# Value projections of a layer ahead of the key and query ones, with the operand splits dealt out anew

## The reference

```python
q = (x @ Wq + bq).reshape(B, T, H, S)        # x is the layer norm of the input
k = (x @ Wk + bk).reshape(B, T, H, S)
v = (x @ Wv + bv).reshape(B, T, H, S)
k = k / jnp.maximum(jnp.linalg.norm(k, axis=-1, keepdims=True), 1e-12)
alpha_val = jax.nn.sigmoid(x @ Walpha + balpha)
beta = jax.nn.softplus(x @ Wbeta + bbeta)
# chunks of 128 tokens: decay masks from cumsum(log(alpha)), attention in a chunk, a state across chunks
...
x = x + attention(layernorm(x))
x = x + down((gelu(gate(y)) * up(y)))        # y = layernorm(x), weights = LUT[codes] * scales
```

## Time and profile before

| quantity | value |
|---|---|
| median of three runs | 1176.11 us |
| profiled execution | 1177.4 us |
| its span (first to last instruction) | 1175.6 us |
| TensorE matmul busy in the span | 1152.5 us, 98% |
| VectorE, ScalarE, POOL busy | 838.0, 394.8, 503.1 us |
| loop T = 4 to 15 of the first stage | from about 13.7 us to 57 us of the span |

### The profile page before, as it was taken

One profiled execution on the slowest core, in us unless ns is written; L12 is line 12 of the kernel. 1 busy time (PEld: TensorE's weight loads), 2 busy tenths in 40 slices (PEclk: granted clock), 3 DMA queues, 4 the chain that ended last, 5 costly groups with the idle time before them and its releaser, 6 DMA issues.

```text
span 1175.6 us, 19512 instructions
## 1 busy us (share of the span) xinstructions
PE 1152.5 (98%) x7756; PEld 757.4 (64%) x7756; DVE 838.0 (71%) x1387; ACT 394.8 (34%) x831; POOL 503.1 (43%) x503
## 2 busy tenths in 40 slices
PE   6999999999989999999999999999999999999998
PEld 3565554656534444777777777777777777777775
DVE  7778554544865664887788778877887787777554
ACT  3343432433332232333333333333333333332221
POOL 3267232322445773425542563366335634462110
PEclk9999999999999999999999999999999999999999
DMA  8012000000010001110011001100110011000111
GB/s 295 2 47 82 22 24 28 19 14 5 20 54 18 19 18 37 33 41 19 19 37 37 19 19 37 37 19 19 37 37 19 19 37 37 19 23 23 37 37 63
DMA packets 22635, 41.94 MB, mean 36 GB/s; under 512 B 2640, under 2 KB 2704, under 8 KB 22544
## 3 DMA queue, kind: packets, MB, share of 16 engines
q1 hardware_dynamic: 22544, 40.70, 10.7%
HBM read 36.46 MB, written 4.23 MB: 35 GB/s over the span
## 4 chain that ended last, share of the span: by engine, by line
PE 90%; DVE 5%; POOL 2%; issue 1%; ACT 1%; DMA 1%; SPq 0%; DVEq 0%; POOLq 0%
PE ps L445 37%; PE ps L472 27%; PE ps L408 14%; PE ps L313 7%; PE ps L282 1%; DVE bigA L774 1%; PE ps L367 1%; POOL WR L1188 1%; DMA WR<-wqkv 1%; PE ps L361 1%; POOL kn_s L1156 1%; PE ps L350 1%; PE ps L374 0%; DVE wf L963 0%; DVE X L887 0%
## 5 line engine op out<-in xcount | busy, mean ns | idle before, releaser
L472 PE MATMUL ps<-WR,ihl_s 128*128 128x512 f16 x816 | 185.9, 379 | 0.0
L408 PE MATMUL ps<-XT,WR 128*128 128x512 f16 x768 | 172.0, 382 | 3.0 <-DVE X L928 3.0
L472 PE MATMUL ps<-WR,vv 128*128 128x512 f16 x720 | 164.7, 379 | 0.0
L445 PE MATMUL ps<-XT,WR 128*128 128x256 f16 x1152 | 157.1, 273 | 0.0
L445 PE MATMUL ps<-REG,WR 128*128 128x256 f16 x1152 | 157.1, 273 | 0.0
L928 DVE SCALAR_TENSOR_TENSOR X<-ps,X 128x512 f32<-128x512 f32 x128 | 88.0, 689 | 79.0 <-PE ps L472 76.9
L408 PEld LDWEIGHTS ps<-XT,WR 128*128 128x128 f16 x768 | 75.4, 98 | 94.7 <-DVE X L928 3.5
L472 PEld LDWEIGHTS ps<-WR,ihl_s 128*128 128x128 f16 x816 | 79.9, 98 | 85.3
L445 PEld LDWEIGHTS ps<-XT,WR 128*128 128x128 f16 x1152 | 112.7, 98 | 33.5
L1172 POOL TENSOR_TENSOR ihl_s<-fw,ihl_s 128x512 f16<-128x512 f32 x51 | 63.5, 1264 | 136.1 <-ACT ihl_s L606 136.1
L445 PEld LDWEIGHTS ps<-REG,WR 128*128 128x128 f16 x1152 | 112.7, 98 | 13.0
(11 more groups left out here) (166 smaller groups left out, 1874.1 us busy)
## 6 DMA issues: line engine op xcount, KB each, us to landing
load<-codes SPq DMA_DIRECT2D x48, 256.0 KB
load<-scales SPq DMA_DIRECT2D x48, 256.0 KB
y<-X SPq DMA_DIRECT2D x16, 256.0 KB, 2.0
bigA<-cla SPq DMA_DIRECT2D x14, 256.0 KB, 3.2
WR<-wqkv SPq DMA_DIRECT2D x3, 1024.0 KB, 10.9
X<-x SPq DMA_DIRECT2D x3, 1024.0 KB, 13.1
X<-x SPq DMA_DIRECT2D x4, 256.0 KB, 3.4
bigC<-bv SPq DMA_DIRECT2D x1, 256.0 KB, 5.8
```

Of the source, the lines that this page charges most:

```text
L408: mm = eng.matmul(bank[:, :], buf[:, wp, o + kt, 128 * j:128 * j + 128], XT[:, xp, kt, 512 * b:512 * b + 512], start=(n == 0), stop=(n == 11))
L445: mm = eng.matmul(half_bank(kind, name), w(wp, kt), x(xp, kt), start=(n == 0), stop=(n == 5))
L472: mm = eng.matmul(PS[bank][:, :], ih[:, ip, 128 * tt:128 * tt + 128], buf[:, wp, 8 + j, :], start=(m == 0), stop=(m == 11))
```

## The change

- The value weights are loaded in four slices, ahead of tiles 2 and 3 of x and of the key weights, each with a semaphore of its own. ScalarE and VectorE split them first.
- TensorE projects the four v tiles of block 0 right after their own turns: turn 0, turn 1, v 0, v 1, turn 2, turn 3, v 2, v 3.
- `QKV_EARLY` keeps 8 entries, k and q of block 0. The steps T = 12 to 15 have no projection. k of head 0 of block 1 moves behind the loop, and k of head 1 takes the place of the fourth v tile in the main loop's first step.
- ScalarE evicts k of block 0 instead of VectorE.
- The split of the query weights goes to POOL: it scales the four slices in place (new line 1152), ScalarE rounds them, and POOL subtracts (new line 1148). Before, VectorE had the subtraction.

```diff
-QKV_EARLY = ([(kind, 0, h) for kind in "kq" for h in range(4)] + [("v", 0, h) for h in range(3)]
-             + [("k", 1, 0)])
+QKV_EARLY = [(kind, 0, h) for kind in "kq" for h in range(4)]
-WORDER = {1: 0, 0: 4, 2: 8}
+WORDER = {2: 0, 1: 4, 0: 8}
...
-    if T + 3 < NT:
+    if T == 0:
+        out.insert(0, ("k", 1, 1))
+    elif T + 3 < NT:
         out.append(("v", (T + 3) // 4, (T + 3) % 4))
...
-                pe.wait_ge(s_hi["n1"], 4 * b + 4)
-                pe.wait_ge(s_lo["n1"], 4 * b + 4)
+                needed = 4 * b + h + 1 if kind == "v" else 4 * b + 4
+                pe.wait_ge(s_hi["n1"], needed)
+                pe.wait_ge(s_lo["n1"], needed)
...
-                    pe.wait_ge(s_wql, WORDER[j] + kt + 1)
+                    if kind == "q":
+                        pe.wait_ge(s_wqlp, kt + 1)
+                    else:
+                        pe.wait_ge(s_wql, WORDER[j] + kt + 1)
...
-            for T in range(4):
+            for T in (0, 2):
                 turn("n1", T)
+                turn("n1", T + 1)
+                qkv("v", 0, T)
+                qkv("v", 0, T + 1)
             for T in range(4, NT):
-                qkv(*QKV_EARLY[T - 4])
+                if T - 4 < len(QKV_EARLY):
+                    qkv(*QKV_EARLY[T - 4])
                 turn("n1", T)
                 logits(T - 4)
             qkv("q", 1, 0)
             for T in range(NT - 4, NT):
                 logits(T)
-            qkv("k", 1, 1)
+            qkv("k", 1, 0)
...
+                elif kind == "k" and b == 0:
+                    ac.wait_ge(s_const, 64)
+                    ac.wait_ge(s_mm["k"], h + 1)
+                    eng.activation(kT[:, 0, h, :], PS[bank_of["k", 0, h]][:, :], ACT.Identity,
+                                   bias=bqk_s[:, 4 + h:5 + h], scale=1.0 / (XS * QS)).then_inc(s_k0, 1)
...
-            for T in range(4):
-                if T == 3:
-                    weights_high(1, range(3))
-                if T >= 1:
-                    turn("n1", T - 1)
-            turn("n1", 3)
-            weights_high(1, [3])
+            weights_high(2, [0, 1])
+            turn("n1", 0)
+            weights_high(2, [2, 3])
+            for T in range(1, 4):
+                turn("n1", T)
             ac.wait_ge(s_const, 64)
             eng.mul(wab_h[:, 0, :, :], wab_f[:, :, :], QS).then_inc(s_wabh, 1)
+            weights_high(1, range(4))
...
-                if T in (5, 9):
-                    weights_high(0 if T == 5 else 2, range(4))
+                if T in (6, 7):
+                    weights_high(0, [2 * T - 12, 2 * T - 11])
                 turn("n1", T)
...
-            for T in range(4):
-                stats("n1", T)
-                if T >= 1:
-                    apply("n1", T - 1)
-                if T >= 2:
-                    turn_low("n1", T - 2)
+            stats("n1", 0)
+            stats("n1", 1)
+            apply("n1", 0)
+            apply("n1", 1)
+            weights_low(2, [0, 1])
+            turn_low("n1", 0)
+            weights_low(2, [2, 3])
+            turn_low("n1", 1)
...
+            project("v", 0, 0)
             turn_low("n1", 2)
             turn_low("n1", 3)
-            weights_low(1, [1, 2, 3])
+            weights_low(1, [0, 1, 2, 3])
+            project("v", 0, 1)
...
+            def weights_low(k):
+                hi, lo = (wq[:, a, k, 0:512] for a in range(2))
+                pl.wait_ge(s_wqh, WORDER[0] + k + 1)
+                eng.tensor_tensor(lo, wsrc[0][:, k, :], hi, ALU.subtract).then_inc(s_wqlp, 1)
+
+            def weights_scaled(k):
+                pl.wait_ge(s_w[0], 16)
+                eng.tensor_scalar(wsrc[0][:, k, :], wsrc[0][:, k, :], QS, None, ALU.mult).then_inc(s_wqs, 1)
...
                 norm_scale("n1", T)
+                if T in (4, 5):
+                    weights_scaled(2 * T - 8)
+                    weights_scaled(2 * T - 7)
+                if T in (7, 8):
+                    weights_low(2 * T - 14)
+                    weights_low(2 * T - 13)
...
                 eng.dma_start(X1[:, T, :], xv[0, :, T, :]).then_inc(s_x[(0, 4, 5, 6)[T]], 16)
+                if T == 1:
+                    for k in range(4):
+                        eng.dma_start(wsrc[2][:, k, :], wv[k, :, 1024:1536]).then_inc(s_wv[k], 16)
             load_w(1)
...
             load_w(0)
-            load_w(2)
```

More of the change, by code:

```diff
@@ L228, in block_kernel @@
         s_w = [sem(f"s_w{j}") for j in range(3)]
+        s_wv = [sem(f"s_wv{k}") for k in range(4)]
+        s_k0, s_wqlp, s_wqs = sem("s_k0"), sem("s_wqlp"), sem("s_wqs")
         s_const, s_out = sem("s_const"), sem("s_out")
@@ L258, in ilo, with evicted @@
             return (s_ilop if on_pool(i) else s_ilov), ILO[i]
+        def evicted(kind, b, h):
+            if kind == "k":
+                return (s_qkv["k"], 4 * b + h - 3) if b else (s_k0, h + 1)
+            return s_qkv[kind], 4 * b + h + 1
         def x1(T):
@@ L297, in qkv @@
             def qkv(kind, b, h):
-                pe.wait_ge(s_hi["n1"], 4 * b + 4)
-                pe.wait_ge(s_lo["n1"], 4 * b + 4)
-                j, done = "qkv".index(kind), 4 * b + h + 1
-                bank = bank_of[kind, b, h] = banks.take(pe, (s_qkv[kind], done))
+                needed = 4 * b + h + 1 if kind == "v" else 4 * b + 4
+                pe.wait_ge(s_hi["n1"], needed)
+                pe.wait_ge(s_lo["n1"], needed)
+                j = "qkv".index(kind)
+                bank = bank_of[kind, b, h] = banks.take(pe, evicted(kind, b, h))
                 n = 0
@@ L336, in head @@
                 pe.wait_ge(s_qkv["q"], 4 * b + 4)
-                pe.wait_ge(s_qkv["k"], 4 * b + 4)
+                pe.wait_ge(*evicted("k", b, 3))
                 free = [(s_ss, T + 1)] + ([(s_kw, 3 * b + c + 1)] if c < 3 else [])
@@ L536, in weights_high @@
             def weights_high(j, ks):
-                ac.wait_ge(s_w[j], 16)
                 for k in ks:
-                    eng.mul(wq[:, 0, k, 512 * j:512 * j + 512], wsrc[j][:, k, :], QS).then_inc(s_wqh, 1)
+                    if j == 0:
+                        ac.wait_ge(s_wqs, k + 1)
+                    else:
+                        ac.wait_ge(s_wv[k] if j == 2 else s_w[j], 16)
+                    eng.mul(wq[:, 0, k, 512 * j:512 * j + 512], wsrc[j][:, k, :], QS if j else 1.0).then_inc(s_wqh, 1)
             def project(kind, b, h):
@@ L622, in dq_mul @@
                     if g == 0:
-                        ac.wait_ge(s_wql, 12)
+                        ac.wait_ge(s_wql, 8)
+                        ac.wait_ge(s_wqlp, 4)
                     if g == 1:
@@ L683, in snapshots @@
                 eng.copy(s5b, half_bank(kind, "P5")).then_inc(s_snap, 1)
-            for T in range(4):
-                if T == 3:
-                    weights_high(1, range(3))
-                if T >= 1:
-                    turn("n1", T - 1)
-            turn("n1", 3)
-            weights_high(1, [3])
+            weights_high(2, [0, 1])
[3 more added lines that the diff above has]
+                turn("n1", T)
             ac.wait_ge(s_const, 64)
             eng.mul(wab_h[:, 0, :, :], wab_f[:, :, :], QS).then_inc(s_wabh, 1)
+            weights_high(1, range(4))
             for T in range(4, NT):
-                if T > 4:
+                if 0 <= T - 5 < len(QKV_EARLY):
                     project(*QKV_EARLY[T - 5])
-                if T in (5, 9):
-                    weights_high(0 if T == 5 else 2, range(4))
+                if T in (6, 7):
+                    weights_high(0, [2 * T - 12, 2 * T - 11])
                 turn("n1", T)
@@ L782, in weights_low @@
             def weights_low(j, ks):
-                dv.wait_ge(s_w[j], 16)
                 for k in ks:
+                    dv.wait_ge(s_wv[k] if j == 2 else s_w[j], 16)
                     hi, lo = (wq[:, a, k, 512 * j:512 * j + 512] for a in range(2))
@@ L797, in project @@
                                              ALU.add).then_inc(s_qkv["v"], 1)
-                elif kind == "k":
+                elif kind == "k" and b >= 1:
                     dv.wait_ge(s_const, 64)
@@ L993, in combine @@
                                   ALU.add).then_inc(s_comb, 1)
-            for T in range(4):
-                stats("n1", T)
-                if T >= 1:
-                    apply("n1", T - 1)
-                if T >= 2:
-                    turn_low("n1", T - 2)
+            stats("n1", 0)
[6 more added lines that the diff above has]
+            turn_low("n1", 1)
+            stats("n1", 2)
+            stats("n1", 3)
+            apply("n1", 2)
             apply("n1", 3)
-            weights_low(1, [0])
+            project("v", 0, 0)
             turn_low("n1", 2)
             turn_low("n1", 3)
-            weights_low(1, [1, 2, 3])
+            weights_low(1, [0, 1, 2, 3])
+            project("v", 0, 1)
             dv.wait_ge(s_const, 64)
@@ L1014, in _ @@
                 apply("n1", T)
[L1015 to L1020, removed]
+                if T < 6:
```

(4 more changed lines are left out.)

## The result

The changed kernel takes 1186.52 us (median of four runs, 1186.16 to 1187.65), against 1175.57 us (median of four, 1174.48 to 1176.43) for the kernel before: 1.009 times as long, 95% interval 1.0076 to 1.0105, some 11 us slower. The forecast was 1186.5. Its profiled execution took 1186.5 us, with a span of 1184.6.

The account below looks back on a forecast made before the run. It took the loop to be bound by TensorE (3.33 us a step) and an equally long ring through three engines (3.32). Terms 6.3 + 1.1 + 3.0 = 10.4 us, added to the median 1176.11, gave 1186.5 us; range 1180.5 to 1190.

Parts of the forecast that it names:

- The front: Start of the kernel up to turn 11: v projections placed ahead make it 7.1 us later; bounds 4.4 and 8.1.
- The ring: Steps T = 12 to 15: waits through three engines keep 3.32 us a step; 12.5 us against 13.3, 0.8 back.
- POOL: Query split on POOL, steps T = 7 and 8: wait 0.85 us plus slowed apply 0.25, 1.1 together; bounds 0 and 2.5.
- The clock: TensorE's clock falls in the thinned tail: turns 0.9 us, projection behind turn 15 2.1, 3.0 in all; bounds 0 and 6.5.
- the wait inside the first q projection: Sign at step T = 8: TensorE waits 0.5 to 1 us on POOL inside that projection.
- the projection behind turn 15: Sign behind the loop: this projection takes 4.5 us or more where it was 2.61; 2.6 would mean the clock holds.
- The delay was passed on behind `head(0)`: Behind the loop: gates, head(0) and all that follows hang on turn 15; everything behind head(0) keeps its old durations.
- the rival "no change": Main loop slack takes up the delay, or a much quicker front nearly balances it: 1176 us, chance 0.04.
- the one in which the clock holds: Tail: TensorE's clock stays up, so 6.3 + 1.1 = 7.4 us slower, 1183.5 us; chance 0.37.
- the one in which the bare steps run at TensorE's pace: Steps T = 12 to 15 take 2.9 us, turn 15 starts at 52.9: faster, 1172.8 us; chance 0.04.
- the one of a queue stuck on POOL: A norm_scale stuck behind query slices loses up to 2.4 us in each of two steps: 1190 us; chance 0.06.

Follow-up runs that it names:

- mix: Against the kernel before: v of two tiles first, two other projections at T = 12 and 13, apply one tile ahead; 1175.28 us, 0.9987 (twelve extra matmuls: 1174.24 us, 0.9981).

## Why the prediction was right

The sum of 10.4 us was made of terms that can be read off one by one, up to the 48 logits, where the trace has 10.1.

- **The front**, forecast 7.1 us. The first v at 9.0 was 9.20, the second's end at 16.9 was 17.00, v 2 at 18.9 was 18.93, and the first k at 24.1 was 24.11. Turn 11 lies 7.77 us later than before; 0.5 of that is POOL's, and 7.2 the front's.
- **The ring**, forecast 12.5 us at the upper clock for the four bare steps. They took 13.18 with turns slowed by 0.45 us at T = 13 and 14, which is 12.3 without that: 1.0 us less than before, where the forecast had 0.8. Opening it took the stretch to 6.4 us and, with POOL out of the way, the ratio to 1.0017: shown by experiment, not only by the rows.
- **POOL**, forecast 1.1 us, is the term that was too large: 0.5 by the trace and by undoing it. The wait in the first q projection was 0.26 us, not 0.85 (the step before had been delayed by 0.26 through an `apply` slowed to 0.80, which gave POOL time). The price of a scaled slice, taken as 1.2 us, was 1.5. Timeline of the changed kernel:

```profile
28.40 3.12 POOL L1152 TENSOR_SCALAR WR<-WR 128x512 f32<-128x512 f32 x2
...
29.38 0.80 DVE L798 TENSOR_SCALAR bigA<-X,mv,rs 128x512 f32<-128x512 f32 x1
```

- **The clock**, forecast 3.0 us with a chance of 0.49. The turns of T = 13, 14 and 15 cost 0.45 us each and the projection 1.8: 3.2, of which the kernel with extra matmuls gave back 2.5 and still met the lower clock once. The prediction took two slowed turns and 2.1 us for the projection. It said that the trace had no stretch like it. It had a relative that was missed: in the kernel before the 120 matmuls behind a wait of 3 us at 326 us were slow, by 1.7 us in all. That row would have raised the chance of this term.
- **No term** had 0.2 us: turn 15 starts with TensorE idle before it, and such a turn takes 0.66 us in the chain instead of 0.44, at the upper clock too (the one at 53.79).

So 7.2 - 1.0 + 0.5 + 3.2 + 0.2 is the 10.1 us at the logits. The near agreement with 10.4 is of three near hits (front, ring, clock) and a POOL term too large by 0.6 us, which the small excesses of the others make up for in part. That the total agrees with 1186.5 to the last digit is luck: the sum was worked out against the profiled execution but added to the median of three, 1.3 us lower, and between the two profiled executions the time grew by 9.1 us only, since that of the kernel before met the lower clock at 326 us. Two of the signs that the prediction named did not come as said: the wait inside the first q projection was to be 0.5 to 1 us, and the projection behind turn 15 took 4.42 us where 4.5 or more was named. The delay was passed on behind `head(0)`, as said, and grew there by 0.5 us. The slack of the rival "no change" does not exist for a delay; but the opposite step does not hold either, as the four projections taken out of the main loop showed.

Of the rivals, the one in which the clock holds fell by the turns of 1.11 us and the projection of 4.42; the one in which the bare steps run at TensorE's pace fell by the ring's rows; the one of a queue stuck on POOL was wrong for this kernel and came true in the kernel with `apply` ahead, where roots and query slices met. The Trainium skill (GPSIMD Engine Reference, Specifications) names contention with VectorE on the shared way in for instructions in a 2-port mode or with two SBUF inputs. The trace agrees in so far as `apply` took 0.80 us instead of 0.53 beside POOL's scaling; whether it runs in such a mode no run shows. The statistics of tile 6 beside the same scaling took their 0.68 us.

## What to carry to other kernels

Before work is moved to an earlier hole, look at what it had been covering: here the projections stood in the shadow of a ring through three engines that was exactly as long as a full step, so taking four of them out shortened the four steps by 1.0 us and left TensorE idle. The length of such a ring is the sum of start-to-start distances in one period, and it is opened by letting the producer's instruction go ahead of the consumer's on the engine that both share. And count TensorE's clock as a cost of idle time: the thinned steps cost 3.2 us beside their own length.

## What the runs showed of the hardware

- After a wait of 3.0 us in otherwise dense work, the next 120 matmuls of 512 columns took 26.07 us in some kernels and executions, and up to 28.96 in others (27.76 in the kernel before). Twelve extra matmuls in the wait took the median of the kernel before down by 0.1%: all its eleven executions had a mean granted clock of 1.000, against eight of 33, and they spread over 1.4 us instead of 3.5. In the version mix the ratio went from 0.9987 to 0.9981, within the intervals, and the eleven executions spread over 3.9 us instead of 2.4.
- In the changed kernel the clock column was 0.67 over 13 us in which TensorE was busy 4.49 us with turns and logits, and 0.58 over the next 5.83 us of full work. At the start of the program it read 1.00 while matmuls took 0.43 us each, so there the durations must be read, not the column.
- POOL scales a float32 slice of 128x512 in place in 1.5 us, and subtracts a float16 one from it in 1.16.
